# Turn lists and PSUM banks of a three-stage decoder kernel laid out anew, with own lists for the first and last three steps

## The reference, cut to what matters

```python
x = _layernorm(x + _L0_attn_ref(x, Wqkv, Wout))              # 16 heads of 32, rotary, causal softmax
x = _layernorm(x + _L0_xattn_ref(x, ctx, ctx, gates, ...))   # mLSTM: 4 heads of 128, gated decay, RMS norm
x = _layernorm(x + _L0_ffn_ref(x, Wq, Wk, Wv, Wr, Wo, ...))  # router picks 4 of 16 heads of 64, softmax
```

## The kernel before, in words

| turn | engine and work |
|---|---|
| a1, a3 / a2, a4 | PE transposes x (line 606) / ACT copies the high part (L960), DVE the low part (L1216) |
| a5 a6, a20 a21, a39 a40, a43 a44 | PE: the four rotary products qk0 to qk3 |
| a7, a8 (a22 a23, a41 a42, a45 a46) | DVE shuffle and cosine (L1226, L1229); POOL sine (L1584), then DVE add (L1233) |
| a9 a10 / a11; a17 a18 / a19 | PE: values v0, v1 / ACT copies them (L967) |
| a12, a24, a52, a72 | PE: scores of four heads into `ps_s` |
| a13 a14, a15 a16 (and later ones) | DVE row maxima (L1240), ACT exponentials (L952) |
| a27 a29 a32 a34, a55 a57 a60 a62, ... | PE transposes of probabilities, `turn` 0 to 15; the next turn copies (ACT L1003 or DVE L1269: a30, a35, a61, a63) |
| a47, a67, a87, a107 | PE: `att` 0 to 3; a48 a50 on ACT, a49 a51 on DVE scale and split them |
| a105, a108, a112, a114 | PE: output projection |
| a113 a115, a116, a117 | DVE residual (L1296), statistics, POOL rstd (L1574), DVE x1 (L1309) |
| b1 b3, b5 b7 | PE transposes ctx and x1; b2 b4 b6 b8 are ACT copies (L1048) |
| b9, b10, b11 | PE gate_t, ACT copy `gate_parts` (L1054), PE gate |
| b12 b13, b14, b15 | DVE gate, ACT exp and ln, DVE log_f |
| b16 b17, b18 b19, b20, b22 b25 | PE cum, DVE; PE a_row, DVE scan and split; PE m_col; PE decay |
| b28 to b34, b36 to b42 | PE: four `c`, four `h` products |
| b44 to b50 | norm chain, mostly DVE; b48 b49 at L1397, L1399, L1203; b50 makes x2 (L1411) |
| c1 c3, c5 | PE transposes x2; PE logit, and POOL adds bo in this turn (`x_bo`, L1635) |
| c6 c7 c8 c9, c10 | router: DVE and ACT; c8 also starts 12 weight DMAs on SP (L573); PE g |
| c15 to c22, c24, c35 | PE: q, k, v products; score pairs |
| c33 c36 c49 c51 | PE transposes `fturn` 0 to 3 (after POOL's L1671) |
| c40 c43, c41 c42 c44 | ACT exponentials; PE fatt0, ACT, DVE split |
| c56 c58, c60 c61 | PE output; norm; ACT y_out and the store |

## Time and profile before

### The profile page before, as it was taken

How to read it: one execution, slowest core, us unless ns; L and a number is a source line. 1 busy time by engine, 2 the same in 40 slices (tenths; PEclk the granted TensorE clock), 3 DMA queues, 4 the chain that set the end, 5 groups by cost and what they waited for, 6 DMA issues and landing times.

```text
span 2551.7 us, 55647 instructions
## 1 busy us (share of the span) xinstructions
PE 2271.7 (89%) x20672; PEld 1861.7 (73%) x20672; DVE 1909.7 (75%) x4586; ACT 1422.9 (56%) x4586; POOL 710.1 (28%) x1069
## 2 busy tenths in 40 slices
PE   5789999999999999999999999999999999999964
PEld 4667777777777777777777777777777777777753
DVE  4567878777778777777877787877777877777753
ACT  4346565556566556565555656555656655656532
POOL 2122323222223322223322222322222332222321
PEclk9899999999999999999999999999999999999976
DMA  4011011111011111011111101111101111111111
GB/s 114 17 43 42 26 43 43 51 51 43 26 43 42 51 51 48 28 44 35 51 51 51 40 28 42 43 51 51 43 26 43 43 51 51 45 33 33 35 34 41
DMA packets 267473, 109.94 MB, mean 43 GB/s; under 512 B 215235, under 2 KB 248259, under 8 KB 267203
## 3 DMA queue, kind: packets, MB, share of 16 engines
q1 hardware_dynamic: 258498, 89.61, 14.1%
q10 hardware_dynamic: 8704, 16.78, 1.7%
HBM read 89.57 MB, written 16.78 MB: 42 GB/s over the span
## 4 chain that ended last, share of the span: by engine, by line
PE 45%; DVE 30%; ACT 10%; issue 10%; POOL 4%; DMA 1%; SPq 1%; POOLq 0%; DVEq 0%; ACTq 0%
PE ps_g L598 36%; PE ps_g L606 7%; ACT p_a L952 4%; DVE neg_max L1240 3%; PE ps_s L598 3%; DVE qk L1233 2%; DVE decay L1368 2%; DVE ctx_t L1399 2%; DVE x_tok L1296 2%; POOL qk_rot L1584 2%; DVE ctx_t L1397 2%; DVE ln_stat_b L1203 2%; DVE ln_stat_a L1203 1%; DVE f_max L1479 1%; ACT p_all L952 1%
## 5 line engine op out<-in xcount | busy, mean ns | idle before, releaser
L952 ACT ACTIVATE p_a<-ps_s,neg_max 128x128 f32<-128x128 f32 (+1 forms) x1024 | 415.2, 443 | 63.5 <-DVE neg_max L1240 63.5
L598 PE MATMUL ps_g<-x_t_hi,wqkv_hi 128*128 128x256 f32 x1024 | 302.3, 295 | 31.5 <-DVE p_t L1269 17.6
L598 PE MATMUL ps_g<-x_t_lo,wqkv_hi 128*128 128x256 f32 x1024 | 287.3, 281 | 0.0
L598 PE MATMUL ps_g<-x_t_hi,wqkv_lo 128*128 128x256 f32 x1024 | 287.2, 280 | 0.0
L1240 DVE TENSOR_REDUCE neg_max<-ps_s 128x2 f32<-128x256 f32 (+1 forms) x512 | 257.2, 543 | 4.5 <-PE ps_s L598 4.5
L1671 POOL TENSOR_SCALAR p_all<-p_all,f_rec,g_bc 128x256 f32<-128x256 f32 x256 | 152.2, 607 | 361.3 <-DVE f_rec L1487 361.3
L1584 POOL TENSOR_TENSOR qk_rot<-qk_rot,const 128x512 f32<-128x512 f32 x128 | 164.6, 1286 | 277.3 <-DVE qk_rot L1226 277.3
L952 ACT ACTIVATION_READ_ACCUMULATOR p_a<-ps_s,neg_max 128x1 f32 x1024 | 234.8, 229 | 0.0
L598 PEld LDWEIGHTS ps_g<-x_t_hi,wqkv_hi 128*128 128x128 f32 x1024 | 195.8, 191 | 44.8 <-DVE p_t L1269 23.7
L1003 ACT COPY p_t<-ps_g 128x384 f32<-128x384 f32 x256 | 119.3, 480 | 193.2 <-PE ps_g L606 190.6
L606 PE MATMUL ps_g<-const,p_a 128*128 128x128 f32 x1536 | 220.9, 281 | 4.2 <-DVE p_t L1269 1.4
(11 more groups left out here) (203 smaller groups left out, 6300.2 us busy)
## 6 DMA issues: line engine op xcount, KB each, us to landing
x_tok<-in_x SPq DMA_DIRECT2D x32, 512.0 KB, 3.6
ctx<-in_ctx SPq DMA_DIRECT2D x64, 256.0 KB, 3.5
p_all<-in_L_ffn_Wq SPq DMA_DIRECT2D x128, 128.0 KB, 2.6
pt_all<-in_L_ffn_Wk SPq DMA_DIRECT2D x128, 128.0 KB, 3.0
y_out<-in_L_ffn_Wv SPq DMA_DIRECT2D x128, 128.0 KB, 3.2
out<-y_out ACTq DMA_DIRECT2D x32, 512.0 KB, 2.8
...
```

The costliest lines, as they stand in the source:

```text
L598: return nc.tensor.matmul(o, l, r, start=first, stop=last)
L952: return nc.scalar.activation(o, i, f, **kw)
```

## The change

Only the order on each engine and the bank of each use change, beside the place of three calls (the tables that DVE makes and POOL's wait for the setup loads now stand at the start of stage b of batch 0). The instructions are the same.

- `FILL` has 512 letters for each engine and takes the place of steps 0, 1 and 2: three a, two b, one c. `ORDER` has 228 letters anew and runs `STEADY` = 28 times. `DRAIN` has 400 letters: one a, two b, three c (the last three steps).
- The stages are now endless streams, so that in `FILL` and `DRAIN` no step border exists.

```diff
+FILL = {
...
+STEADY = NB - 4
...
-            for s in range(NB + 2):
-                in_turns(s, engine, {"a": stage_a, "b": stage_b, "c": stage_c})
-
-    def in_turns(s, engine, stages):
-        live = {n: stages[n](s - lag) for lag, n in enumerate("abc") if 0 <= s - lag < NB}
-        for n in ORDER[engine]:
-            if n in live:
-                next(live[n])
-        for n, g in live.items():
-            assert next(g, "end") == "end", "ORDER leaves work undone"
+            in_turns(engine, {"a": stage_a, "b": stage_b, "c": stage_c})
+
+    def in_turns(engine, stages):
+        def stream(n):
+            for b in range(NB):
+                yield from stages[n](b)
+
+        live = {n: stream(n) for n in "abc"}
+        for n in FILL[engine] + ORDER[engine] * STEADY + DRAIN[engine]:
+            next(live[n])
...
         def stage_b(b):
+            if not b:
+                tables()
...
         def stage_b(b):
+            pool.wait_ge(setup_loaded.sem, SETUP)
...
 BANKS = {
-    "v": "32", "turn": "2322213123011203", "ctx": "22", "x1": "33", "gate_t": "0", "decay": "10", "h": "1203",
-    "vf": "1", "fs": "0310", "fturn": "3332", "x": "32", "qk": "2312", "att": "2003", "out": "12", "gate": "2",
-    "cum": "3", "a_row": "1", "m_col": "0", "c": "2103", "x2": "01", "logit": "3", "g": "3", "q": "2", "k": "0",
-    "fatt": "31", "wo": "23",
+    "a_row": "0", "att": "0203", "c": "0210", "ctx": "21", "cum": "2", "decay": "20", "fatt": "21", "fs": "3113",
+    "fturn": "3213", "g": "3", "gate": "0", "gate_t": "0", "h": "1303", "k": "0", "logit": "3", "m_col": "0",
+    "out": "10", "q": "2", "qk": "2102", "turn": "1302102202301203", "v": "13", "vf": "1", "wo": "13", "x": "32",
+    "x1": "10", "x2": "03",
 }
```

More of the change, by code:

```diff
@@ L38 @@
+        "cbbaacbb"
     ),
     "scalar": (
-        "caaabcbbbaaabcbbaacbbccbbabbcabaaababbbbcaaabacbaabcbabbcbcbcbbabaccbabaacbbccbbbbbbcbbacbbcbaaabaccabaacaccac"
-        "ccaacaacaccaccaacaccacaccacaaacaaaccaaaaaacaaacccaccaaaaaccaaaacaaaacaaaaaaaaacaaabaaaacaaabaabaaacaacacaaaaaa"
-        "aaaaacaa"
+        "cabbabcababbcbccbbbbbbbcabababaacaababaabcbabbbcbbabcbaaabcbbcbababbcbbbabaacbabaacbbcccccccbaccaaacacaaaacaca"
+        "aacaccaaccaaacacacccccacacaaacaaaaaaaaaaaaacccccaacccacacaaaaacaaaaaaaaaaaaaaaaaaaaaaaaaaaaaaaaacacccbacccabab"
@@ L43 @@
+        "aababaab"
     ),
     "vector": (
-        "abaaababbbcccbccaacbcbaabbacbbaabbbcbababacabbabbbabaabbbcaabbbbbbbbbcaabbbbcbabbbccbabbacccccccacaacbbccaaaac"
-        "acaaccaccaaaccacccaaacccacaacaccaaaacaacaaacacaaacaccaaacabcaacaaaaaacaacaaaaaaacaaaacaacaaaaaaaaaaaaacaaaaaaa"
-        "caaaaaaa"
+        "aaaabbccbbcbbabbbbbaccacbbbcbbaabaacababaaaabaabaacabbbbbbbbbbbabaccbbbcbbcbcacbbbcbbbcaaabaaaccaccccabcbabcac"
+        "aaccaacaaccaccccaaacccaaaaacccccacaaaaacacaaacacacaacccaaacaaaacaaaacaaaaaaaaaaaacccaacaaaaaaaaaaaaaaaacacaaaa"
@@ L53 @@
+        "cacaabca"
     ),
     "sync": (
-        "cccbbbbacabaaaaaabccbaaccaaaaaaaaaaacaaabababacacacaacabaabaacbbcabcccaacbaaacaaaccacaaaacaaabaaaaabbcbccccaaa"
-        "aabcacacaaabaacaacaabcbaabbccaacaacabbaaabcccccabbaaaabcbbbaacacaaaccababbaaaaaabbbcbcaabccbacbcbbacacaababccc"
-        "abaacaaa"
+        "aaccbcbaaccccbaabbaccbacbbaccabcaaaaaaaaacaaaaaacaaccaaaaaaccacaaaaacaacabcbcaaccaccaaaaaaaababbaaabaccaaabbbc"
+        "abacccabbababcbaaacabaaaabacccacbbcabacbcacabaaaaaacababbbccabaabbbaacccaaacbaababbcbaaaabbaccaccabbcabacaaaaa"
@@ new lines @@
+        "acbacaac"
+    ),
+}
+DRAIN = {
+    "tensor": (
+        "ababbcaabcbcbaabbabbbcabcaaabaabbacabbccaabbabbbbaacbbbabcacbbcbbbabbabbbbabbacbacabcacccacaccccaaacbaaabaccac"
+        "aaccacaccacacaacacaaaccacacbccaccaccaaaaaacacaaccaaacaaaacabcbacaaaacaaaaaaacaacaacaaacaaabaaabaaaaacaaaaaaaaa"
+        "acababcbcabccbbbbcbbbccbbbbbbbbcbcbbbabbbbcbcccbbbcabbbbbbcbcbbbcbbcccccccccccbcccccccbcbcccccbccccccbcccccccc"
+        "cccccccccccccccccccccccbcccccccccccccccbccccccccccccccccccccbccccccccc"
+    ),
+    "scalar": (
+        "acbcbacbbabababcbbacacbbabcbaabaabbabacaabccbabcabbababbabbcbaaccbbbbacccbacbbababbbbccaaaabbcbbccccbaaacccaaa"
+        "ccccabcaaaaaaccaccaaaccacaccaabaaccccaacaaaaaacaccacaaaaccaaaaacccaaacaaaaacaaaaaaaaaacbaabaaaaaaaaaaaaaaaaaba"
+        "cbaacbcccbcbbbbcabcbcbbbbbcbabbabbbbbbbbbccbbbcbcbbcbcbcbbbcabbccbcbcbbccbcbcccccccbccccccccccccccbccccccccccc"
+        "cccccbccccccccccccccbccccccccccccccbcccccccccccccccccccccccccccccccccc"
+    ),
+    "vector": (
+        "aaabbbbcbaacaccaababbccbcbabbbbbcaaabbbaabbbaabababbbacabbabbbabbbabbabccbcaabcabbcbbbbcacccabacbcaacbacbcccac"
+        "aacaaaccaaaccaccccacccacaaccccaaaacaaaaacacaccacaaacaaabcaacacaacaaaaaacaacaabaabaaacaacacbaabababaaaaabaaabaa"
+        "caaababaacaaaaacaaccacbcccbbbbbcbbbbbbbcbbbbbcbcbbbbcbbbbcbbbccbccbbbcbcccccbccccccbccccccbcccccccccccccccbccc"
+        "cccccccccbcccccccccccccccccccccccccccccccccccccccccccccccccccccccccccc"
+    ),
+    "gpsimd": (
+        "cabaaaabcbbacabbbacbabbbcbbabbbabcccbabaabbababbaababacaabcccbabbbaabaaabcbbcaacacbcbcabcbacbbbaaaaccbcbcaacab"
+        "cccbcacbcaacacaacaaacaaaaaaaaaaaabaacaaacacaacaaacaccaaaaaacccacaaaccccaccaaaaaaacaaaaacbcacabaaaacacacacbcaac"
+        "abaaababbabacbcabbcbbccbcabbccbbbcbbbcbbccccbcbbbcbccbcbbccbcbbcbbabbccbbbcbbbbcccbbbccbcccccccccccccccccccccc"
+        "bccccccccccbcccccccccccccccccccccccccccccccccccccccccccccccccccccccccc"
+    ),
+    "sync": (
+        "baaaaaabaacaaabacccaabaabacaaaaacaaaccbbcbbacccbaaaaaaaabacabacabaacabaacaccaaaacabaccbbcaccaacbcaaacaaaaaacbc"
+        "ccabcaabaaaabaacaccacbccbcaaccbbaaccaccabcaaababbbaabbaacacabacbabaaaaccaabbcbacbcaaaabacbabcaaacbbcabccbcaaba"
+        "acbacccacacbbbaabcccbbbcccbcccbcbbcbbcccccbbbcccbcbbbcccccbbcbcccbbcbbccbcbcccbccccccccccccbbbbcccbccbccbcbbcc"
+        "ccccbcccbccbccccbcccccccbccccccccbccccbcbbccbccccccccccccccbcccccccbcc"
@@ L503, in plan @@
             done = 0
-            for s in range(NB + 2):
-                in_turns(s, engine, {"a": stage_a, "b": stage_b, "c": stage_c})
-    def in_turns(s, engine, stages):
-        live = {n: stages[n](s - lag) for lag, n in enumerate("abc") if 0 <= s - lag < NB}
-        for n in ORDER[engine]:
-            if n in live:
-                next(live[n])
-        for n, g in live.items():
-            assert next(g, "end") == "end", "ORDER leaves work undone"
+            in_turns(engine, {"a": stage_a, "b": stage_b, "c": stage_c})
[6 more added lines that the diff above has]
+            next(live[n])
+        for g in live.values():
+            assert next(g, "end") == "end", "the lists leave work undone"
     plan()
@@ L588, in sync @@
                 engine.dma_start(dst, src).then_inc(setup_loaded.sem, 16)
-        for s in range(NB + 2):
-            in_turns(s, "sync", {"a": stage_a, "b": stage_b, "c": stage_c})
+        in_turns("sync", {"a": stage_a, "b": stage_b, "c": stage_c})
         sp.wait_ge(*out_stored(NB - 1))
@@ L943, in tensor @@
         pe.wait_ge(first_loaded.sem, FIRST)
-        for s in range(NB + 2):
-            in_turns(s, "tensor", {"a": stage_a, "b": stage_b, "c": stage_c})
+        in_turns("tensor", {"a": stage_a, "b": stage_b, "c": stage_c})
     def scalar(engine):
@@ L1193, in scalar @@
         act.wait_ge(first_loaded.sem, FIRST)
-        for s in range(NB + 2):
-            in_turns(s, "scalar", {"a": stage_a, "b": stage_b, "c": stage_c})
+        in_turns("scalar", {"a": stage_a, "b": stage_b, "c": stage_c})
     def vector(engine):
@@ L1558, in vector @@
         dve.wait_ge(wqkv_split.sem, QKV_PIECES)
[L1559 to L1562, removed]
+        in_turns("vector", {"a": stage_a, "b": stage_b, "c": stage_c})
     def gpsimd(engine):
@@ L1701, in gpsimd @@
         pool.wait_ge(half_ready.sem, 6)
[L1702 to L1705, removed]
+        in_turns("gpsimd", {"a": stage_a, "b": stage_b, "c": stage_c})
     with nc.Block() as block:
```

47 lines of the change are left out of this document (41 added, 6 removed).

## The result

The changed kernel takes 2526.23 us (median of 4 runs, 2524.98 to 2527.24), against 2557.39 for the kernel before on the same chip: a ratio of 0.9873 (0.9859 to 0.9886). It is 31 us faster; 68 were forecast. The sign was right, the size was not.

What follows compares the result with a forecast made beforehand. TensorE, busy 89% of the span, was taken as the bound, so only its idle could go: 48 us in 30 full steps, 14 in the first two, 6 in the last two, 68 off 2557.1 for 2489; range 2455 to 2540.

Steps and rivals of the forecast that it cites:

- The 5.80 us stay. Gain 0.: Start of a full step: a5 still comes 5.80 us after a1, set by the norm chain, despite new banks; gain 0.
- c41 behind a52, cost 0.73: Full step: c41 one score block later, so idle before a72 grows from 1.48 to 2.21 us; cost 0.73.
- Turn 7's price of 0: Full step: turn 7 follows turn 6 in the same bank, but inside the wait before a72; cost 0.
- the waits of b16, a43 and the six small ones: TensorE waits within a full step would go: gains 1.04 us (b16), 0.45 (a43) and 1.18 (six small ones).
- b11: Full step: b11 now follows b9 with only c5 between, too short for b10's copy; cost 0.15 us (bounds 0 and 0.5).
- the 2.6 of idle at the start, and so the 6.75: TensorE idle as read in the kernel before: 2.6 us at a full step's start, 6.75 in the whole step.
- The clash rival: a8 on DVE waits behind both GpSimd additions of c5, 0.4 us too late a step: time 2501; chance 5%.
- the parts given for it (1.7, 4.7, 1.5 and 4.5): Step 1 gains: stage a bank waits 1.7 us, earlier tables 4.7, granted clock 1.5, a35's copy before b48 and b49 4.5.
- Step 0: Stage a alone: bank waits of att0 and turn 3's neighbour go, turn 7 costs about 0.7; gain 1.7 us.
- the full step's gain: 1.6 us a step, claimed for 28 steps of `ORDER` and about for the full steps in `FILL` and `DRAIN`.
- The last steps: Last two steps: gain 4 us from b48 and b49 moved, 3 from c30's router earlier, cost 1 from b50; sum 6.
- c31 itself is a serial chain and stays: Last sequence's stage c, alone at the end: unchanged, 48 to 49 us from its loads.

Runs made afterwards that it cites:

- experiment 5: Changed kernel with c41 ahead of a52 again in TensorE's `ORDER`, nothing else: 2507.88 us, ratio 0.9809 to the kernel before.
- experiment 1: Changed kernel with 16 useless identity transposes on TensorE in each step before its wait for x1: 2487.61 us, ratio 0.9734 to the kernel before.
- experiment 6: Changed kernel with c41 ahead of a52 and 16 identity transposes before the wait for x1: 2474.87 us; with 8 transposes instead: 2473.63 us.
- experiment 4: Changed kernel with turn 7 in bank 3 instead of bank 2: 2527.80 us, ratio 0.9888 to the kernel before.
- experiment 7: Kernel before with b12 and b13 (and b11, no work there) ahead of c8 in DVE's `ORDER`: 2536.90 us, ratio 0.9920.
- x7: Changed kernel (new banks, new lists for first and last three steps) with the old list in the 28 steps between: 2631.04 us, ratio 1.0292 to before.
- experiment 3: Kernel before with one digit changed, the second ctx transpose in bank 1 instead of bank 2: 2566.24 us, ratio 1.0038.

## Why the prediction was right and wrong

**The step that failed** is the first term of the full step: "The 5.80 us stay. Gain 0." The duration did stay, from the first transposes at 1119.18 to a5 at 1124.94 are 5.76. But the bank waits that were taken away had split the idle before the norm chain's end into 0.73, 0.68 and 0.36; without them it is one piece of 2.16, and the clock falls behind it. The sum counted idle only, and took the granted clock, 1.00 in the earlier trace rows, as given. It was in the prediction as a matter of step 1 alone. A fall at the start costs 1.6 us by the two steps of experiment 5, the second one about 1.2 (the changed kernel's steps take 75.6 on average with both and 74.7 with the first alone, some of these with another wait of 0.5). With 27 and 12 falls that makes some 2.0 us a step, 57 in all, as an estimate; experiments 1, 5 and 6 show that with both falls removed the new order, c41 in its old place, gives 51 us more.

**c41 behind a52, cost 0.73: wrong, and so was its reason.** The idle of a60, a62 and c49 is 1.53, that with a72 at most 1.69, not 2.21, and its releasers are DVE's `x_t_lo`, the copy p_t and GpSimd's `p_all`, not ScalarE's queue before a72. Experiment 5 shows no idle lost by the place of c41, but 18 us, and with them the falls of the clock that went. I had read the idle before a72 as the sum of a fixed ScalarE queue. Turn 7's price of 0 there was right (experiment 4).

**Right:** the waits of b16, a43 and the six small ones are gone, as idle. The term of b16 by itself is 0.79 of the 1.04 predicted (experiment 7). b11 shows no wait: its 0.15 was at the lower bound. With c41's cost mis-sized as well, the idle fell by 1.96 instead of 1.6; so the idle was sized nearly right. The full step without a fall takes 73.1 (experiment 5), 2.7 less than before: 1.7 of it idle and 1.0 shorter busy time, which the sum didn't have and of which no run gives the cause; the clock took some 2.0 of the 2.7 back, and 0.73 a step was left. One reading was too high and cost nothing: the 2.6 of idle at the start, and so the 6.75, should be 1.77 (0.73, 0.68 and 0.36) and about 5.9, as the 75.80 less 69.84 of the earlier trace rows say. The clash rival did not come: a8 stands behind b15 and takes 0.68.

**The first steps.** Step 1 shrank by 11.65; the parts given for it (1.7, 4.7, 1.5 and 4.5) make 12.4. The waits of 6.03 and 4.38 went, and 2.81 came in the place of the second, behind x1, in the same way as the full step's 2.16. Step 0 gave 0.35 and not 1.7. The 1.81 of the earlier trace rows is gone, but two waits of 1.16 came where the kernel before has none, the wait of the second `r_wide` product grew from 0.89 to 1.66, and 0.57 for a copy stands again at another place (timeline of TensorE in step 0; that the new banks are the reason was not tested):

```profile
54.41 0.87 PE L680 MATMUL ps_g<-const,p_a 128*128 128x128 f32 x6 [1.16 <-DVE att_s L1358]
55.85 0.73 PE L680 MATMUL ps_g<-const,p_a 128*128 128x128 f32 x3 [0.57 <-ACT p_t L1076]
...
58.24 0.69 PE L680 MATMUL ps_g<-const,r_wide 128*128 128x128 f32 x2 [1.66 <-DVE p_t L1341]
...
68.60 0.85 PE L680 MATMUL ps_g<-const,p_a 128*128 128x128 f32 x6 [1.16 <-DVE att_s L1358]
```

Step 2 became 1.9 longer instead of 1.6 shorter. Its clock is 1.00 and its busy time 70.21; the 7.4 of idle against 5.8 are new waits of a list of its own. I had taken over the full step's gain for it unread.

**The last steps: 6 predicted, none came.** c30's DVE chain did get its turns ahead of batch 31's, and from its weight loads to its store it still takes 51.5 us (2410.44 to 2461.91), before 50.4 (2443.41 to 2493.77). c31 is longer, 49.5 (2470.55 to 2520.01) against 46.1. Its timeline shows two waits that were not there before, for a copy in the same bank (`"fs": "3113"`: fs1 has the bank of vf, fs3 that of fturn 0), 1.65 in all:

```profile
2489.32 1.13 PE L672 MATMUL ps_g<-k_f,q_f 64*128 64x256 f32 x8 [0.77 <-ACT v_f L1195]
...
2496.17 2.08 PE L672 MATMUL ps_g<-k_f,q_f 64*128 64x256 f32 x8 [0.88 <-DVE pt_all L1570]
```

"c31 itself is a serial chain and stays" left out that its banks changed. The rest of the 3.3 goes with a TensorE that is 1.58 us longer busy from the first product with the loaded weights to the end of the span (27.19 from 2477.42 on, against 25.61 from 2509.05 on in the kernel before, 132 instructions each) at a mean clock of 0.65 against 0.70; no run separates these. The order of the ends as such was worth about what was said: 20 predicted, 21 to 23 measured with the banks held the same, once the 5 us of x7 that lie between the ends are taken off. The new banks took part of it back at the ends.

**Open.** What decides whether the clock falls is bounded, not settled. It did not in 0.73, 0.68 and 0.36 within 3.5 us (before) nor in 0.73 and 0.33 around 1.1 us of work (experiment 6); it did in 9 of 28 steps at 1.65 in one piece (experiment 3), in 12 of 28 at 0.35, 0.78 and 0.40 within 2.6 us and in only 7 at the same three pieces in experiment 1, and in 27 (changed kernel) and 23 (experiment 5) of 28 at 2.15. So equal idle can be followed by a fall in one step and by none in the next: in these runs falls are more frequent where the piece is longer, and something else, which no run shows, decides the single step. A new bank for c31 alone was not tried either.
